# A four-layer conditioned transformer kernel: the first layer's experts on sorted tiles of 512 tokens

## What is computed

```python
xn = _modulate(_ln(x), sh_mlp, sc_mlp)
xf = xn.reshape(-1, C)
gate_logits = xf @ w_gate
topk_logits, topk_idx = jax.lax.top_k(gate_logits, TOP_K)      # TOP_K = 2 of 4 experts
gates = jax.nn.softmax(topk_logits, axis=-1)
cw = jnp.sum(jax.nn.one_hot(topk_idx, NUM_EXPERTS, dtype=xf.dtype) * gates[..., None], axis=1)
hmid = jax.nn.gelu(jnp.einsum('tc,ech->eth', xf, w1) + b1[:, None, :], approximate=True)
eo = jnp.einsum('eth,ehc->etc', hmid, w2) + b2[:, None, :]
moe = jnp.einsum('te,etc->tc', cw, eo).reshape(B, N, C)
return x + g_mlp[:, None, :] * moe
```

## Time and profile before

| | us |
|---|---|
| runs | 1791.73, 1783.18, 1787.73 |
| median | 1787.73 |
| profiled execution | 1783.59 |
| its span | 1781.3 |

### The profile page before, as it was taken

The page is one execution under the profiler, slowest core; times in us unless marked ns, Lnnn a source line. Parts: engine busy times, 40 slices in busy tenths (PEclk is TensorE's granted clock), DMA queues, the critical chain, the costliest instruction groups (busy, mean ns, idle before and its releaser), DMA issues.

```text
span 1781.3 us, 29668 instructions
## 1 busy us (share of the span) xinstructions
PE 1655.9 (93%) x9774; PEld 1098.1 (62%) x9774; DVE 1370.6 (77%) x2543; ACT 847.9 (48%) x1554; POOL 669.3 (38%) x1528
## 2 busy tenths in 40 slices
PE   6989998799999999999998999889998999989998
PEld 4732233688898888888773222478886222348885
DVE  7688886888988756757978888677797888876763
ACT  4647776333412211211555777732355677762222
POOL 0566665766767666666766640000000000000000
PEclk9999999999999999999999999999999899999999
DMA  6563334301410131211264323110006222400001
GB/s 168 136 156 86 85 84 78 75 4 25 109 30 4 7 75 6 42 6 5 49 171 111 79 76 111 34 38 1 14 19 195 79 72 72 129 1 1 1 1 54
DMA packets 79139, 110.70 MB, mean 62 GB/s; under 512 B 28032, under 2 KB 61678, under 8 KB 78889
## 3 DMA queue, kind: packets, MB, share of 16 engines
q1 hardware_dynamic: 76970, 104.96, 19.6%
q0 software_dynamic: 2048, 4.21, 5.5%
HBM read 81.02 MB, written 23.71 MB: 59 GB/s over the span
## 4 chain that ended last, share of the span: by engine, by line
PE 65%; DVE 24%; issue 4%; DMA 3%; ACT 2%; SPq 2%; DVEq 0%; ACTq 0%
PE psum L965 20%; PE psum L1228 13%; PE psum L1114 9%; PE psum L1103 9%; PE psum L1089 7%; DVE minus_max L1537 3%; DVE hid_lo L1715 2%; PE psum L1030 2%; DVE bn L1445 2%; DVE hid_hi L1714 2%; DVE branch L1736 1%; PE psum L1253 1%; DVE x_norm L1467 1%; DMA k_stack<-qk_parts_d 1%; DVE residual L1738 1%
## 5 line engine op out<-in xcount | busy, mean ns | idle before, releaser
L1537 DVE TENSOR_REDUCE minus_max<-psum 128x2 bf16<-128x1024 f32 x384 | 452.8, 1219 | 77.1 <-PE psum L1089 70.1
L868 ACT ACTIVATE probs<-psum 128x512 f32<-128x512 f32 x768 | 418.6, 600 | 150.7 <-PE psum L1103 148.1
L914 ACT ACTIVATE hid_f<-psum 128x512 f32<-128x512 f32 x216 | 129.2, 598 | 545.4 <-PE psum L965 516.0
L965 PE MATMUL psum<-x_split,w_hi 128*128 128x512 f32 x864 | 317.5, 408 | 13.6 <-DVE x_tail L1484 5.9
L1228 PE MATMUL psum<-w_hi,hid_hi 128*128 128x288 f32 x864 | 259.6, 300 | 14.7 <-DVE hid_lo L1715 10.3
L1103 PE MATMUL psum<-q_stack,k_stack 109*128 109x512 bf16 x768 | 259.9, 385 | 8.2 <-ACT probs L868 5.3
L1228 PE MATMUL psum<-w_hi,hid_lo 128*128 128x288 f32 x864 | 255.9, 296 | 0.0
L1228 PE MATMUL psum<-w_lo,hid_hi 128*128 128x288 f32 x864 | 255.7, 296 | 0.0
L1089 PE MATMUL psum<-k_stack,q_stack 108*128 108x512 bf16 x720 | 221.3, 389 | 11.8 <-DVE minus_max L1537 8.6
L1103 PEld LDWEIGHTS psum<-q_stack,k_stack 109*128 109x128 bf16 x768 | 72.5, 97 | 244.2 <-ACT probs L868 178.1
L693 POOL TENSOR_TENSOR qr_m<-qr_m 64x8 f32<-64x8 f32 (+35 forms) x544 | 205.9, 378 | 42.6
(11 more groups left out here) (263 smaller groups left out, 2513.4 us busy)
## 6 DMA issues: line engine op xcount, KB each, us to landing
qk_parts_d<-qk_parts SPq DMA_DIRECT2D x36, 384.0 KB, 4.2
q_stack<-qk_parts_d SPq DMA_DIRECT2D x48, 216.0 KB
k_stack<-qk_parts_d SPq DMA_DIRECT2D x48, 216.0 KB
q_stack<-qk_parts_d SPq DMA_DIRECT2D x48, 144.0 KB
k_stack<-qk_parts_d SPq DMA_DIRECT2D x48, 144.0 KB
raw_b<-in_L_cond_w SPq DMA_DIRECT2D x5, 1296.0 KB
raw_a<-in_L_cond_w SPq DMA_DIRECT2D x5, 1152.0 KB
q_stack<-qk_parts_d SPq DMA_DIRECT2D x48, 72.0 KB
```

What stands on the lines that cost most here:

```text
L868: act.activation(PE_[:, v // 4, v % 4, :], psum[:, score_bank(v), :], ACT.Exp, scale=SCALE).then_inc(s_e, 1)
L914: act.activation(HF[:, i % 2, :], bk(i % 2), ACT.Gelu_apprx_tanh).then_inc(s_g, 1)
L965: i = pe.matmul(dst, a, r, start=(n == 0), stop=(n == len(terms) - 1))
L1537: dve.tensor_reduce(MX[:, g % 2, 2 * u:2 * u + 2], psum[:, o:o + 2, :], AX.X, ALU.max, negate=True).then_inc(s_mx, 1)
```

## The change

The rows that an expert works on become its own tokens only. A token's slot in its expert's list is its rank there; the lists are cut into tiles of 512 rows, at most eleven in all (4096 pairs of token and expert, and a part of a tile for each expert but one), and each tile is worked on like a batch: nine units, with the weights of its expert.

- Constants: `SETS` loses layer 0's four sets; `TILES = 2 * TOK // N + EXPERTS - 1` (11), 99 units in place of 144.
- Rows: `modulate_rows` makes the modulated rows in token order (two passes over four tiles of 128 tokens), `turn_x`, `copy_x`, `logits`, `turn_logits` and `gate_ranks` give each token its two experts, `ranks` counts with small matmuls how many tokens of each expert are ahead, and `slots` makes two row numbers for each token.
- `moe()` on TensorE, ScalarE and VectorE begins with 19 steps of these and of the end of attention (`FRONT`), with no unit beside them. Then come the tile table, tile 0's turn, and the loop of 99 units.
- GpSimd: after 12 reflectors it waits for the slots and scatters 4 x 8 times 128 rows of 352 floats to DRAM; after 16 more reflectors it waits for the tiles' results and gathers 4 x 4 rows of 288 floats twice: the first experts' results once tile 9 is stored, the second ones' once tile 10 is. The other 36 reflectors follow.
- SP: clears the scattered area in 16 DMAs in layer 0's attention; reads each tile's start and expert from the table into registers; loads each tile's rows and, in thirds, its expert's w1 and w2; stores each result.
- Every tile's weights are split anew (`tile_pieces`: in each unit one tile of w1 and one of w2). Skew entries lie in units 9 to 40, steps of the exponential in units 66 to 94.
- VectorE adds the results with `combine(k, b)`: k = 0 in the last tile's units 5 to 8, k = 1 at the start of layer 1, whose normalising and turning come after it, as in layer 0.
- The modulation of layer 0's feed-forward part is made as rows (nine matmuls of 288 columns in place of 39 small ones) and stored to DRAM.

```diff
-SETS = [(0, e) for e in range(EXPERTS)] + [(1, 0), (2, 0)]
+SETS = [(1, 0), (2, 0)]
+TILES = 2 * TOK // N + EXPERTS - 1
+MOE_UNITS = TILES * HM
+MOE_ROWS = (EXPERTS * TOK) + 3 * N
+SKEW_UNIT, EXPM_UNIT = 9, 66
+FRONT_SKEW = 4
+FRONT = 11 + 2 * FRONT_SKEW
+PIVOTS = (0, 12, 28, 64)
...
+            def moe_loads():
+
+                sp.wait_ge(s_tb, 1)
+                e = tile_expert(1)
+                load_tile_b2(1, e)
+                for i in range(3):
+                    load_tile_w1(1, i, e)
+                sp.wait_ge(s_sd, 32 * 16)
+                load_rows(0)
+                load_rows(1)
+                for i in range(3):
+                    load_tile_w2(1, i, e)
...
+                for t in range(TILES):
+                    if t >= 1:
+                        store_tile(t - 1)
+                        if t + 1 < TILES:
+                            e = tile_expert(t + 1)
+                            load_tile_b2(t + 1, e)
+                            load_tile_w2(t + 1, 2, e)
+                    if t + 2 < TILES:
+                        e = tile_expert(t + 2)
+                        load_tile_w1(t + 2, 0, e)
+                        load_rows(t + 2)
+                        load_tile_w2(t + 2, 0, e)
+                        load_tile_w1(t + 2, 1, e)
+                        load_tile_w2(t + 2, 1, e)
+                        load_tile_w1(t + 2, 2, e)
...
+            def scatter(b):
+                if b == 0:
+                    gp.wait_ge(s_zr, 16 * B * HG)
+                gp.wait_ge(s_ix, b + 1)
+                for t in range(TT):
+                    for k in range(2):
+                        gp.indirect_dma_start(out=XSD[:, :], out_offset=bass.IndirectOffsetOnAxis(ap=IDX[:, TT * b + t, k:k + 1], axis=0),
+                                              in_=XMR[b][:, t, :], in_offset=None).then_inc(s_sd, 16)
+
+            def gather(k, b):
+                if k == 1:
+                    gp.wait_ge(s_cb, b + 1)
+                for t in range(TT):
+                    gp.indirect_dma_start(out=YG[b][:, t, :], out_offset=None, in_=YD[0:N * (TILES - 1 + k), :],
+                                          in_offset=bass.IndirectOffsetOnAxis(ap=IDY[:, TT * b + t, k:k + 1], axis=0)).then_inc(s_gk[k][b], 16)
+
             gp.wait_ge(s_pt, 1)
-            for k in range(D3):
+            for k in range(PIVOTS[0], PIVOTS[1]):
+                reflector(k)
+            route_constants()
+            for b in range(B):
+                scatter(b)
+            for k in range(PIVOTS[1], PIVOTS[2]):
+                reflector(k)
+            gp.wait_ge(m_y, 16 * (TILES - 1))
+            gp.wait_ge(s_iy, 1)
+            for b in range(B):
+                gather(0, b)
+            gp.wait_ge(m_y, 16 * TILES)
+            for b in range(B):
+                gather(1, b)
+            for k in range(PIVOTS[2], PIVOTS[3]):
                 reflector(k)
...
+            def moe():
+
+                for step in range(FRONT):
+                    for b in range(B):
+                        k = step + 8 if b == 0 else step - FRONT_SKEW * (b - 1)
+                        if k in (0, 1):
+                            turn_o(0, b, 2 * k)
+                            turn_o(0, b, 2 * k + 1)
+                        elif k == 2:
+                            turn(0, 1, b, (0, 1))
+                        elif k == 3:
+                            turn(0, 1, b, (2,))
+                        elif k in (4, 5):
+                            proj(0, b, 2 * (k - 4))
+                            proj(0, b, 2 * (k - 4) + 1)
+                        elif k == 7:
+                            turn_x(b)
+                        elif k == 8:
+                            logits(b)
+                        elif k == 9:
+                            turn_logits(b)
+                        elif k == 10:
+                            ranks(b)
+                for c in range(KC + 1):
+                    turn_tile(0, c)
+                for j in range(MOE_UNITS + 2):
+                    t, m = divmod(j, HM)
+                    if j < MOE_UNITS:
+                        tile_hidden(j)
+                    if j >= 2:
+                        tile_second(j - 2)
+                    if t + 1 < TILES and 2 <= m <= 2 + KC:
+                        turn_tile(t + 1, m - 2)
+                    if 0 <= j - EXPM_UNIT < EXPM_STEPS:
+                        expm_step(j - EXPM_UNIT)
...
+            def combine(k, b):
+
+                dve.wait_ge(s_gk[k][b], 16 * TT)
+                if (k, b) == (0, 0):
+                    dve.wait_ge(s_gl, 16)
+                for t in range(TT):
+                    i = dve.scalar_tensor_tensor(YG[b][:, t, :], YG[b][:, t, :], LG[:, TT * b + t, k:k + 1], GMLP[:, b, :], ALU.mult, ALU.mult)
+                link(i)
+                rows = XR[:, TT * b:TT * b + TT, :]
+                dve.tensor_tensor(rows, rows, YG[b][:, :, :], ALU.add).then_inc(s_cb, 1)
+                dve.wait_ge(s_cb, B * k + b + 1)
...
+                elif l == 1:
+                    for b in range(2):
+                        combine(1, b)
+                        stats(b, l, 0)
+                        normalise(l, 0, b)
+                    low(l, 0, 0)
+                    combine(1, 2)
+                    stats(2, l, 0)
+                    low(l, 0, 1)
+                    qkv(l, 0, lambda m: normalise(l, 0, 2) if m == KC else None)
+                    combine(1, 3)
+                    stats(3, l, 0)
+                    low(l, 0, 2)
+                    normalise(l, 0, 3)
+                    qkv(l, 1)
+                    low(l, 0, 3)
+                    qkv(l, 2)
```

775 lines of the change are left out of this document (583 added, 192 removed).

## The result

The changed kernel takes 1857.67 us (median of 4 runs, 1856.44 to 1860.04), the kernel before 1785.49 in the same comparison (4 runs): ratio 1.040, 95% interval 1.037 to 1.043. It is 72 us slower. The forecast was 24 us slower, with 1855 as the upper end of the range: the sign was right and the size was not.

A forecast was written before the change was run, and what follows sets the result against it. TensorE, busy 93% of the span, was taken as the bound; front 105, wait 31, tiles 403 and tail 34 made 573 against 566.5 us, +7, with 13 and 4 more +24: 1808 us, range 1762 to 1855.

The forecast's parts named there:

- What is removed: Layer 0's experts: 144 units become 99, taking 45 x 3.21 = 144 us off TensorE.
- Front: Layer 0's experts, 19 steps before any unit, until every token has its slot: 105 us, ends 88 and 118.
- Last slot to first hidden product: Tile table, scatters, row loads and turns before tile 0's first hidden product: 31 us, ends 24 and 45.
- Tiles: The eleven tiles: 403 us, TensorE's 371 plus 21 for VectorE's skew phase, 6 and 5; ends 376 and 430.
- 29 exponential steps x 1.25: Matrix exponential steps within the eleven tiles: 36 us of TensorE's 371.
- Tail: Last second product to layer 1's first qkv product, with store, gather, combine and normalising: 34 us, ends 27 and 45.
- Layer 1's start: Layer 1's first qkv product to first probabilities: 87 us against 74.1, so +13, ends +5 and +18.
- The rest: Clearing DMAs beside layer 0's attention (0 to 5) and reflectors 28 to 63 beside layers 1 and 2: +4, -3 to 10.
- Slow indirect DMAs: Rival: scatters and gathers at 3 us each, where VectorE casts and copies, giving 1848 us; chance 0.15.
- Weights per tile: Rival: each tile's 4.4 MB of loads and stores binds, the stage some 50 us longer, 1858 us; chance 0.05.
- Covers that hold: Rival: upper clock in front, steps near VectorE's floor, front 88, wait 25, tiles 390, tail 29, giving 1761 us; chance 0.27.
- The forecast's own signs: First gelu near 450, front clock 0.5 to 0.7, units 4.0 us in tiles 1 to 4, 4.6 with exponential step.

The follow-up runs named there:

- the combined version: Changed kernel with take ahead of weight parts, skew placing by GpSimd, front offset three, four clearing DMAs in attention, twelve in the front: 1797.86 us, ratio 1.009.
- the version with an offset of three: Changed kernel with batches set off by three steps in place of four in the front (17 steps, not 19): 1842.63 us, ratio 1.031.

## Why the prediction was right or wrong

**What is removed: right.** There are 171 gelus in place of 216, and a plain tile takes 30.8 us: six units at 3.2, two at 3.66 and one, with the take, at 4.26.

**Front: right in kind, 10 us too high.** It took 95 us against 105, within the ends 88 and 118. The granted clock was 0.69 over it; the 105 had assumed the lower level throughout. The sum is better than its parts, and so partly luck: the slots of batches 1, 2 and 3 came 53, 76 and 95 us into the front, where the working had 67, 93 and 105. The first chain was 14 us shorter than laid out, and the last one, alone, took 19 us in place of 12.5.

**Last slot to first hidden product: right in the sum.** It took 29 us against 31. A scatter stands at 0.96 us of GpSimd (956 to 1518 ns) and 1.26 from one to the next, against 1.3 taken, and all eight were issued 11.5 us after the last slot. The rows' loads were issued only after 17.3 us where 13 to 15 were forecast, since SP's 18 loads took 9.5 us in place of 7. The rows then landed in 4.4 us (7 forecast), the turns took 7.6 (6.5 forecast), and the last 2.5 us of the forecast were not needed.

**Tiles: the step that failed.** Forecast 403, measured 442. The sum of TensorE's work (371) was right: the combined version, at a granted clock of 0.98, has it busy for 367 us over its tiles. The size of VectorE's loss in the skew phase was right too, and its form was not: 24 us in tiles 2 to 4 against 21, but as one wait for the take, with lost clock behind it, and not in each unit. Tile 1, with a skew step in each of its units, lost nothing. (By the working's own parts, 3.8 us and a tenth more, it would have been 4.2 us a unit and 26 us.) Two things were not in the sum at all:
- Some 15 us by tile 7 (55.9 against 38.5 us once the placing was moved, of which 2 came back in tile 6). The step that failed said "29 exponential steps x 1.25" and took the first one's input for granted, a wait priced at nothing. The row to look at was SP's 63 issues, 39.4 us of its queue with 17 us to spare in the kernel before, and the change fills that queue with 24 DMAs a tile. The working followed SP's queue for the first tile's rows and not for this step.
- 11 to 13 us in the last tile. No row of before could show it; it needs the gathers, and came in three of six groups of runs. What else it needs stays open.
What is left, some 9 us, is in small terms that were not taken apart, such as plain tiles at 31 us in place of 30.5.

**Tail: 7 us too low, within its ends.** It took 41 us against 34. VectorE's part was right, 22.5 us against 22. Ahead of it the take was done 3.8 us after the last second product and its store landed 3.6 later (4 forecast for both), and the first four gathers took 11.0 us from their first issue to their landing in place of 7.5.

**Layer 1's start: near, for a reason that is partly open.** It took +15 against +13. Without any reflectors beside it it took 82.0 us, 5 below the 87 of the forecast; but the kernel before had reflectors there too, so they don't explain the +15.

**The rest: both halves too small.** The clearing DMAs were taken at 2 us with bounds 0 to 5, "its stacks come two groups ahead". Measured: the last probabilities 14 us later in the changed kernel, and +18 us in time when the sixteen were added alone to the kernel before. The step that failed is the bound: being two groups ahead was taken as cover without asking how long one clearing DMA holds the queue. 0.86 MB at the 190 GB/s that the runs show is 4.5 us, 16 of them 72 us, ahead of loads for which TensorE already waited 1.2 and 1.0 us in the kernel before. The reflectors were taken at 2 us with bounds -3 to 10. From layer 1's first probabilities to layer 2 the versions with them took 369.7 to 376.9 us in 17 traces, and the one without them 363.9: 6 to 13 us. The forecast said that reflectors 28 to 63 ran beside layer 0 before; of these, eleven already ran beside layer 1. (The lower ends of the terms add up to 1734 us and not to 1731, which changes nothing.)

**Rivals.** *Slow indirect DMAs* didn't come, at the size that was priced. The 32 gathers stand at 942 to 1135 ns in the changed kernel, but the first 16 of them ran beside the stop, with VectorE nearly idle. In traces without the stop, where VectorE works beside them, three to five of the first 16 take 1.2 to 1.95 us each, and from the first to the last one it is 21 to 22 us in place of 19. One of the slow ones, in the version with an offset of three:

```profile
856.85 1.95 POOL L930 DMA_INDIRECT moe_y<-moe_out_d,row_places  x1 [0.30 <-issue]
```

The Trainium skill, SBUF — State Buffer, "A bandwidth-pool intuition that's wrong (but worth ruling out)", has 3100 ns in place of 620 for a DMA that GpSimd issues while VectorE copies. No indirect DMA here takes that long; that some are slower beside a working VectorE agrees with it in kind. There are single operations of VectorE at twice their usual duration (0.98 us at 527.73 for a part that takes 0.42 elsewhere); what holds them is not shown. *Weights per tile* didn't bind: no wait for `w1` or `w2` stands among TensorE's, at 114 GB/s over the tiles. *Covers that hold* came true in part of the front, and it was not enough.

**The forecast's own signs.** The first gelu near 450 came at 454.4, and it would have come near 444 without the 10 us from attention. The clock of 0.5 to 0.7 was 0.50 to 0.69, and units with an exponential step stood at 4.5 against 4.6. The units of the skew phase, forecast at 4.0, stood at 3.2 to 3.8 with one of 11 to 13 in each tile: the forecast had named 3.4 there as a sign that it is wrong, and as a statement on single units it was. A lag on an in-order engine is paid at the point where the other side needs it, not evenly.

## What to carry to other kernels

Taking work off TensorE pays only if what was covered by it stays covered: here 144 us of products turned into 165 us of front, wait and tail, and much of the rest was queues. When a change fills a DMA queue, go through every small DMA already in it and its due time, and price a bulk transfer by how long it holds the queue against the slack of the load behind it; the same 13.7 MB cost 18 us in attention, 9 to 16 in the front and 57 in the qkv stage, by what stood behind them, and 1 to 3 us when a quarter stood in attention and the rest in the front. Where a product waits for banks to be emptied, look at what stands ahead of the emptying, since the wait is paid a second time in the clock; moving it forward gave 5 us in the trace here. And compare a change of a few us only with a run on the same chip: the offset of three looked like 5 us against another chip's trace and was 1 to 2 us.
